# A two-layer perceiver on one core: the first cross attention begins in another order of keys, values, looks and norms

## The reference

```
x = x + _L0_xattn_ref(_layernorm(x, axis=-1), ctx_768, ...)       # x (16, 64, 256), ctx_768 (16, 1601, 192)

q = (x @ wq + bq).reshape(B, SQ, 16, 16);  k = (y @ wk + bk)...;  v = (y @ wv + bv)...
scores = jnp.einsum('bqhd,bkhd->bhqk', q, k) / jnp.sqrt(jnp.asarray(D_HEAD, x.dtype))
attn = jax.nn.softmax(scores, axis=-1)
out = jnp.einsum('bhqk,bkhd->bqhd', attn, v).reshape(B, SQ, D_EMBED);  return out @ wo + bo
```

## Time and profile before

| | |
|---|---|
| median of 3 runs | 1882.81 us (1880.94 to 1883.79) |
| span of the profiled execution | 1878.6 us |
| busy over the span | TensorE 96%, VectorE 68%, ScalarE 50%, GpSimd 49% |
| first scores of TensorE (round 0) | 45.64 us |

### The profile page before, as it was taken

How to read it: one execution, slowest core, us unless ns; L and a number is a source line. 1 busy time by engine, 2 the same in 40 slices (tenths; PEclk the granted TensorE clock), 3 DMA queues, 4 the chain that set the end, 5 groups by cost and what they waited for, 6 DMA issues and landing times.

```text
span 1878.6 us, 44195 instructions
## 1 busy us (share of the span) xinstructions
PE 1804.1 (96%) x17738; PEld 1528.4 (81%) x17738; DVE 1280.6 (68%) x2720; ACT 942.6 (50%) x2050; POOL 912.6 (49%) x1183
## 2 busy tenths in 40 slices
PE   6999999999999999999999999999999999899998
PEld 5778878887887778889999999999999967656665
DVE  6888888888888877667676666676676736652222
ACT  3676766766667745454444444444444424512221
POOL 5877777777777517455433433333333214412322
PEclk9999999999999999999999999999999999999999
DMA  5112111121110110133222222232222024141110
GB/s 161 37 48 61 37 38 37 38 67 42 37 37 3 58 50 1 58 94 105 62 62 62 62 62 62 75 86 76 73 62 62 1 97 199 36 159 29 25 32 13
DMA packets 50747, 113.08 MB, mean 60 GB/s; under 512 B 4929, under 2 KB 37265, under 8 KB 49009
## 3 DMA queue, kind: packets, MB, share of 16 engines
q1 hardware_dynamic: 46128, 105.13, 18.9%
q0 software_dynamic: 4416, 5.12, 1.6%
HBM read 105.78 MB, written 5.37 MB: 59 GB/s over the span
## 4 chain that ended last, share of the span: by engine, by line
PE 79%; DVE 10%; ACT 6%; issue 3%; DMA 2%; SPq 0%; POOL 0%; POOLq 0%; DVEq 0%; ACTq 0%
PE ps L104 8%; PE ps L164 8%; PE ps L2650 6%; PE ps L500 5%; PE ps L481 5%; PE ps L1715 5%; PE ps L458 4%; PE ps L2674 3%; PE ps L475 2%; PE ps L1716 2%; PE ps L410 2%; DVE arena L1827 2%; PE ps L1702 2%; PE ps L1705 2%; PE ps L1704 2%
## 5 line engine op out<-in xcount | busy, mean ns | idle before, releaser
L574 DVE TENSOR_REDUCE arena<-ps 128x1 f32<-128x400 f32 (+1 forms) x512 | 257.6, 565 | 84.7 <-PE ps L458 84.3
L729 ACT ACTIVATE arena<-ps 128x384 f32<-128x384 f32 (+1 forms) x512 | 223.3, 524 | 94.3 <-PE ps L481 93.9
L1715 PE MATMUL ps<-arenaR 128*128 128x386 f32 x768 | 242.9, 374 | 1.1 <-DVE arenaR L1821 1.1
L813 POOL TENSOR_TENSOR arena<-arena 128x512 f32<-128x512 f32 (+1 forms) x152 | 196.6, 1294 | 81.6 <-ACT arena L729 74.2
L1931 ACT CAST arenaR<-ps 128x512 fp32r<-128x512 f32 (+1 forms) x256 | 116.8, 509 | 199.6 <-PE ps L164 198.7
L1716 PE MATMUL ps<-arenaR 128*128 128x194 f32 x768 | 194.2, 253 | 0.0
L1821 DVE TENSOR_TENSOR arenaR<-ps,arenaR 128x512 fp32r<-128x512 f32 (+1 forms) x256 | 138.9, 585 | 28.4 <-ACT arenaR L1931 28.4
L1716 PEld LDWEIGHTS ps<-arenaR 128*128 128x128 f32 x768 | 147.5, 192 | 0.0
L1956 ACT ACTIVATE wsb<-ps,arena 128x1200 f32<-128x1200 f32 x64 | 80.9, 1265 | 131.4 <-DVE arena L1880 131.4
L1715 PEld LDWEIGHTS ps<-arenaR 128*128 128x128 f32 x768 | 145.5, 189 | 1.4 <-DVE arenaR L1821 1.4
L1827 DVE TENSOR_REDUCE arena<-ps 128x1 f32<-128x400 f32 (+1 forms) x256 | 137.1, 566 | 0.6 <-PE ps L1705 0.6
(11 more groups left out here) (374 smaller groups left out, 4948.6 us busy)
## 6 DMA issues: line engine op xcount, KB each, us to landing
wsb<-in_ctx SPq DMA_DIRECT2D x16, 1152.0 KB
wsb<-in_ctxT SPq DMA_DIRECT2D x16, 800.5 KB, 5.0
wsb<-in_ctxT SPq DMA_DIRECT2D x32, 400.2 KB, 7.5
gu<-in_m_gu SPq DMA_DIRECT2D x8, 1536.0 KB, 19.2
arena<-in_ctxT SPq DMA_DIRECT2D x15, 800.5 KB, 5.3
arena<-in_ctxT SPq DMA_DIRECT2D x30, 400.2 KB, 7.4
dn<-in_m_dn SPq DMA_DIRECT2D x8, 768.0 KB, 11.4
wsb<-in_f_w SPq DMA_DIRECT2D x2, 1024.0 KB, 6.0
```

Of the source, the lines that this page charges most:

```text
L574: e.tensor_reduce(mx4[n % 2][:, u, i:i + 1], ps[:, at("look", n, i, u), 0:400 + (i == 3)], AX.X, ALU.max).then_inc(c.maxed.at((n, i, u)), 1)
L729: e.activation(v[:, u, 0:128 * GN[s]], ps[:, at("st", n, s, u), 0:128 * GN[s]], ACT.Exp).then_inc(c.exp_a.at((x0, n, s, u)), 1)
L813: e.tensor_tensor(sums_p[0:k], sums_p[0:k], v[0:k, :, 128 * t:128 * t + 128], ALU.add).then_inc(added_p.at((n, s)), 1)
L1715: e.matmul(o, PTh[:, t, :], v[:, t, 0:386], start=(t == 0), stop=False)
```

## The change

All of it is in `latents`. FIRST is gone: the rounds begin at 0, and what stood in the rounds -3 to -1 is written out ahead of the loop, in another order on each engine.

- VectorE alone makes the low parts of the first context: `first_low(i)` has both differences, and VectorE makes block 0 before the norm of tile 0, block 1 before the first queries, 2 and 3 after them. GpSimd's loop over L837 is gone. It makes the diagonal blocks of passes 0 and 1 and then three splits of context 1.
- TensorE: keys of both head groups for block 0, then the queries; the looks stand between keys and values of the first context instead of in pairs.
- `norms = {2 * t - 2: t ...}`: tile t is normed in round 2t - 2 (0, 2, ..., 12). The bias is added tile by tile, by GpSimd in the rounds 1, 3, ..., 15.
- SP: seven tiles of x (896 KB) are loaded behind the first part of `load_raw(1)` instead of ahead of it.

```diff
-    norms = {-3: (1, 2, 3), -2: (4, 5), -1: (6, 7)}
+    norms = {2 * t - 2: t for t in range(1, NT)}
...
-    for i in range(4):
-        at("k", 0, i)
-    at("h", 0)
-    at("q", 0)
-    for i in range(2):
-        at("v", 0, i)
-    for r in range(FIRST, LAST + 1):
+    for use in (("k", 0, 0), ("h", 0), ("k", 1, 0), ("q", 0), ("v", 0, 0), ("k", 0, 1), ("v", 0, 1), ("k", 0, 2)):
+        at(*use)
+    at_look(0, 0)
...
+    for r in range(LAST + 1):
...
-        e.dma_start(c.x[:, 1:NT, :], x[:, 1:NT, :]).then_inc(c.in_x.at("x", 16), 16)
...
         load_raw(1)
+        e.dma_start(c.x[:, 1:NT, :], x[:, 1:NT, :]).then_inc(c.in_x.at("x", 16), 16)
...
     def pe(e, w):
-        for i in range(4):
-            keys(0, i)
+        keys(0, 0)
         turn_h(0)
+        keys(1, 0)
         queries(0)
-        for i in range(2):
-            vals(0, i)
-        for r in range(FIRST, LAST + 1):
+        vals(0, 0)
+        keys(0, 1)
+        vals(0, 1)
+        keys(0, 2)
+        look_at(0, 0)
+        keys(0, 3)
+        look_at(0, 1)
+        vals(0, 2)
+        look_at(0, 2)
+        vals(0, 3)
+        look_at(0, 3)
+        vals(0, 4)
+        keys(1, 1)
+        keys(1, 2)
+        turn_m(0)
+        keys(1, 3)
+        look_at(1, 0)
+        vals(0, 5)
+        look_at(1, 1)
+        vals(0, 6)
+        for r in range(LAST + 1):
...
     def dve(e, w):
+        def first_low(i):
+            k = slice(400 * i, 400 * i + 400 + (i == 3))
+            lo = c2[0][64:128, k]
+            w.wait_ge(*c.split_hi((x0, 0, i, 1)))
+            e.tensor_tensor(c1l[0][:, k], raw1[0][:, k], c1h[0][:, k], ALU.subtract).then_inc(c.dv.at(), 1)
+            w.wait_ge(*c.split_hi((x0, 0, i)))
+            e.tensor_tensor(lo, raw2[0][64:128, k], lo, ALU.subtract).then_inc(c.dv.at(("first low", i)), 1)
...
-            w.wait_ge(*c.biased(x0))
+            w.wait_ge(*c.biased((x0, tile)))
...
+        first_low(0)
         norm_tile(c, e, w, "in", 0)
+        first_low(1)
+        queries(0)
+        first_low(2)
+        first_low(3)
+        w.wait_ge(*padded("rows"))
         for i in range(4):
+            maxima(0, i)
+        maximum(0)
+        for i in range(2):
+            maxima(1, i)
+        for r in range(LAST + 1):
...
-            for t in norms.get(r, ()):
-                norm_tile(c, e, w, "in", t)
+            if r in norms:
+                norm_tile(c, e, w, "in", norms[r])
...
     def pool(e, w):
-        for i in range(4):
-            k = slice(400 * i, 400 * i + 400 + (i == 3))
-            w.wait_ge(*c.split_hi((x0, 0, i, 1)))
-            e.tensor_tensor(c1l[0][:, k], raw1[0][:, k], c1h[0][:, k], ALU.subtract).then_inc(c.split_lo.at((x0, 0, i)), 1)
         blockdiag(0)
-        for r in range(FIRST, LAST + 1):
+        blockdiag(1)
+        for i in range(3):
+            split(1, i)
+        for r in range(LAST + 1):
...
-            if r == -1:
+            if r % 2 and r // 2 < NT:
+                t = r // 2
                 w.wait_ge(*c.in_bias[0]("in"))
-                w.wait_ge(*c.normed(("in", NT - 1)))
-                e.tensor_tensor(c.x[:, :, :], c.x[:, :, :], c.biasb[:, :].unsqueeze(1).broadcast_to([128, NT, D]),
-                                ALU.add).then_inc(c.biased.at(x0), 1)
+                w.wait_ge(*c.normed(("in", t)))
+                e.tensor_tensor(c.x[:, t, :], c.x[:, t, :], c.biasb[:, :], ALU.add).then_inc(c.biased.at((x0, t)), 1)
```

More of the change, by code:

```diff
@@ L233, in latents @@
     G0, GN = (0, 4, 7, 10), (4, 3, 3, 3)
-    FIRST, LAST = -3, 2 * N
+    LAST = 2 * N
     w_hi = c.w_hi
@@ L305, in at, with at_look @@
         return bank[use]
-    for i in range(4):
-        at("k", 0, i)
-    at("h", 0)
-    at("q", 0)
-    for i in range(2):
-        at("v", 0, i)
-    for r in range(FIRST, LAST + 1):
+    def at_look(n, i):
+        for u in range(4):
+            at("look", n, i, u)
+    for use in (("k", 0, 0), ("h", 0), ("k", 1, 0), ("q", 0), ("v", 0, 0), ("k", 0, 1), ("v", 0, 1), ("k", 0, 2)):
+        at(*use)
+    at_look(0, 0)
+    at("k", 0, 3)
+    at_look(0, 1)
+    at("v", 0, 2)
+    at_look(0, 2)
+    at("v", 0, 3)
+    at_look(0, 3)
+    for use in (("v", 0, 4), ("k", 1, 1), ("k", 1, 2), ("m", 0), ("k", 1, 3)):
+        at(*use)
+    at_look(1, 0)
+    at("v", 0, 5)
+    at_look(1, 1)
+    at("v", 0, 6)
+    for r in range(LAST + 1):
         for i in range(2):
@@ L317, in latents @@
                     at("st", n, s, u)
-            for n, k in looks(r)[i:i + 1]:
-                for u in range(4):
-                    at("look", n, k, u)
+            for use in looks(r)[i:i + 1]:
+                at_look(*use)
             if r >= 1 and i == late(r):
@@ L371, in load_raw @@
                 w.wait_ge(*c.split_hi((x0, b - 2, 3)))
-                w.wait_ge(*c.split_lo((x0, b - 2, 3)))
-            if b == 2:
-                w.wait_ge(*c.dv(("first low", 3)))
+                w.wait_ge(*(c.split_lo((x0, b - 2, 3)) if b > 2 else c.dv(("first low", 3))))
             e.dma_start(raw1[b % 2], d["ctxT"][b, 0:128, :]).then_inc(in_ctx[b % 2].at(None, 16), 16)
@@ L398, in split_done @@
             w.wait_ge(*c.split_hi((x0, b, i)))
-            w.wait_ge(*c.split_lo((x0, b, i)))
-            if b == 0:
-                w.wait_ge(*c.dv(("first low", i)))
+            w.wait_ge(*(c.split_lo((x0, b, i)) if b else c.dv(("first low", i))))
         def keys(n, i):
@@ L642, in dve @@
             e.tensor_tensor(wl[k], W[k], wh[k], ALU.subtract).then_inc(c.dv.at(("weight low", k)), 1)
+        first_low(0)
         norm_tile(c, e, w, "in", 0)
-        for i in range(4):
-            k = slice(400 * i, 400 * i + 400 + (i == 3))
[L646 to L650, removed]
-        for r in range(FIRST, LAST + 1):
+        first_low(1)
[3 more added lines that the diff above has]
+        w.wait_ge(*padded("rows"))
+        for i in range(4):
+            maxima(0, i)
[3 more added lines that the diff above has]
+        for r in range(LAST + 1):
             if asks(r - 1) is not None:
@@ L655, in dve @@
                 project(projects(r - 1))
-            for t in norms.get(r, ()):
+            if r in norms:
                 w.wait_ge(*c.in_x("x"))
-                moments(c, e, w, "in", t)
+                moments(c, e, w, "in", norms[r])
             for use in looks(r)[:1]:
@@ L747, in act @@
             e.copy(wh[k], W[k]).then_inc(w_hi.at(k), 1)
-        for i in range(4):
-            split(0, i)
-        for i in range(4):
-            keys(0, i)
+        split(0, 0)
+        keys(0, 0)
         take_h(0)
-        for i in range(2):
-            vals(0, i)
-        for r in range(FIRST, LAST + 1):
+        keys(1, 0)
+        split(0, 1)
+        split(0, 2)
+        vals(0, 0)
+        split(0, 3)
+        keys(0, 1)
+        vals(0, 1)
+        keys(0, 2)
+        keys(0, 3)
+        for i in range(2, 5):
+            vals(0, i)
+        for i in range(1, 3):
+            keys(1, i)
+        split(1, 0)
+        turn_m(0)
+        keys(1, 3)
+        split(1, 1)
+        vals(0, 5)
+        split(1, 2)
+        vals(0, 6)
+        for r in range(LAST + 1):
             for use in groups(r)[:1]:
```

4 lines of the change are left out of this document (2 added, 2 removed).

## The result

The changed kernel takes 1886.53 us (median of 19 runs, 1880.85 to 1890.68) against 1882.56 (19 runs of the kernel before). The ratio is 1.002, 95% interval 1.0011 to 1.0029: about 4 us slower, small but not zero. The time lies in the predicted range (1876.5 to 1887.5), but the forecast of no change was wrong. The profiled execution has a span of 1882.6 us, 4.0 over the span before, so the trace can be read against it.

A forecast was written before the change was run, and what follows sets the result against it. TensorE was taken to bound the rounds, with idle time in the beginning. A gain of 10.2 us and a loss of 10.0 (6.6 + 2.4 + 1.0) gave -0.2, so 1882.6 us, range 1876.5 to 1887.5.

The forecast's parts named there:

- the forecast of no change: Whole kernel: gain and loss within 3.8 us of each other, 0.2%; the forecast itself, chance 0.53.
- (1): Beginning: VectorE makes all eight first low parts, about 0.5 us each without GpSimd beside it, off the path.
- (2): Beginning: TensorE's queries, now third, wait for wo, landing 7.0 us after issue, at 14.2 us.
- Step (3): Beginning: TensorE's work from the queries to its first scores takes 19.6 us at full clock; first scores at 35.4.
- The slow stretch: Beginning: 3.5 us of TensorE at half speed, as before the change, cost about 1.6 us more.
- the bound of 37.5: Beginning: latest first scores if the slow stretch lasts twice as long with 0.5 us of waits; gain 8.1.
- My reading of the chain: Beginning: TensorE's 2.97 us gap ends with looks standing nearly alone; the new order can fill that idle time.
- the wait for the root: Odd rounds: norm waits for GpSimd's root, delaying TensorE's second scores 0.7 to 1.5 us, middle 1.1, six times: 6.6.
- VectorE's lag: Rounds: VectorE's lateness carried through odd into even rounds, 0 to 1.1 us, middle 0.6, four times: 2.4.
- The rule weighed there: Rounds: started first, the norm keeps 0.41, wait 0.7 a round; by the profile row 1.5; the middle was taken.
- The dear norm: Rounds: norm always stretched to 1.22 and lag handed on; loss from 14, +5.4, 1888.2 us; chance 0.15.
- The clock in the waits: Rounds: TensorE's clock falls in waits, 1.6 us a time, more than once; waits here under 2; chance 0.03.

The follow-up runs named there:

- e6: Changed kernel, but GpSimd makes the low part of the first context again, as before; 1884.41 us in one execution.
- e3: Kernel before with its own beginning; only norms of tiles 1 to 7 and bias additions moved into the rounds; 1890.84 us, ratio 1.0036 to before.
- e9: Kernel before with its own beginning, norms in the rounds as changed, GpSimd's root first in the even round; 1879.65 us, ratio 0.998 to before.
- e12: Changed kernel with GpSimd's root at the head of the even round, run a second time; 1874.36 us, ratio 0.995 to before.
- e2: Changed kernel, but GpSimd makes the root first in the even round, ahead of its additions and scale; 1872.89 us, ratio 0.9946 to before.
- e5: Changed kernel, but GpSimd makes the next context's low parts ahead of the root in the even round; 1909.69 us in one execution.
- e10: Changed kernel, but the norms of tiles 1 to 7 write 32 of 256 columns; 1887.57 us, ratio 0.9999 to before.
- e14: Changed kernel, but GpSimd's first subtraction of the split waits for the norm; 1882.34 us, ratio 0.9998 to before.
- e8: Changed kernel with GpSimd's root first in the even round and TensorE's values of block 0 ahead of the first queries; 1874.16 us, ratio 0.9953 to before.

## Why the prediction was wrong

It forecast -10.2 + 10.0 = -0.2; the traces show -7.9 + 11.7 = +3.8. Both halves went the way the steps said; the gain was 2.3 too large and the loss 1.7 too small.

**Steps (1) and (2), the low parts and the queries.** The mechanism was right: low parts of 0.57 to 0.66 each instead of 1.26, and queries that wait for wo. That the low parts are off the path holds up to the queries; behind them e6 leaves it open. wo landed 7.8 us after its issue instead of 7.0: 0.9 of the missing gain. Over all the kernels it took 6.7 to 8.9, also with the transfers of before (6.7 in e3, 7.6 in e9), so one trace gave it to within 2 us at best.

**Step (3), 19.6 us of TensorE's work.** Mis-sized. At full clock it is 21.03 (e12): two looks with a pair of values between are 2.27 apart, not 0.85 + 1.2. I took half of a row of two looks less its end, but a look that stands alone between other products has 0.95 in its row. 1.4 of the missing gain. The slow stretch was put at 1.6 and is that, 22.61 against 21.03; that is luck in part, since over the seven profiles it costs 0 to 2.6. 15.09 + 22.61 gives 37.70, just outside the bound of 37.5.

**What made the beginning slow before.** My reading of the chain was wrong, without harm for the number. I laid the gap before 33.37 to looks whose maxima stand alone, and said that the new order fills it. Most of it was VectorE's norms between the maxima: 5.0 to 6.0 us are had by moving the norms alone (e3, e9). The chain of waits named only the maxima, since they ended last.

**The rounds: the wait for the root.** The mechanism was right to the step (root behind scale, norm, maxima, bank, second scores), and e2 and e5 move it both ways. The term was too small. I took the middle, 1.1, between a norm of 0.41 and one of 1.22; the odd rounds from 3 to 13 have the upper end, 1.60, or more, because the norm always starts in the same moment as GpSimd's subtraction and waits for all of it. The seven odd rounds' delays of the second scores sum to 11.25 instead of 6.6: five rounds of 1.6 to 2.0, round 3 with 2.55 for three small operations behind the norm, which I had counted at a part of 1 us, and round 1, where I had none, with 0.28.

**The rounds: VectorE's lag.** Too dear: 2.4 and 1.0 stood in the sum, and 0.5 came (11.74 less 11.25). I take it that VectorE's lateness is mostly TensorE's too, and that the idle time of the even rounds takes the rest; no run tests that by itself. In the changed kernel no even round's second scores are late (3.86 to 3.88).

**The rule weighed there.** By the Trainium skill ("SBUF — State Buffer", "Who interferes with whom") whoever issues first keeps the shared ports and the other blocks for the whole instruction. The traces agree with the second half (e10: 32 columns, 1.11, till the end of GpSimd's operation; e14: without the overlap 0.41). They speak against the first half, for this pair, if the start in the trace is the issue: VectorE's norm started 0.04 ahead and was the one that stood. Whether the ports are taken in the moment that the trace calls the start, no run here tells. The row had shown the same, and by the row alone the term was 6 x 1.5 = 9.0 in place of 6.6 and the sum +2.2: the right sign, though still within 0.2%. Taking a middle between a row and a rule that the row speaks against cost 2.4 of the 4.0 us by which the sum was off.

**The rivals.** The forecast itself asked for gain and loss within 3.8 us of each other, and they came out 3.8 apart. The dear norm, given 0.15, came by half: the norm is always 1.22, but the lag isn't handed on, only round 3 loses over 2.3, and the loss is 11.7 and not over 14. The clock in the waits, given 0.03, was judged too cheaply: waits of 2.5 us are in round 3, not under 2 as I wrote, and the clock fell there in five of seven profiles, though not in the one that the sum was compared with. So no rival came whole. The sum was off by 4.0: the gain was put 2.3 too large and the loss 1.7 too small, the latter being a wait put 4.65 too small against a lag put 2.9 too large.

## What to carry to other kernels

Before moving work out of a stage that idles into one that is bound, find what the moved instruction waits for there, and move that first: here six tiny GpSimd operations at the head of their round instead of behind a division turned 0.2% slower into 0.5% faster. Where one operation of another engine ends a wait and the next one of that engine is long, as the root and the subtraction here, the two collided every time, so the bad end of the range was the likely one, not the middle. When a chain names an operation that is always there (the maxima), look at what stands on the same engine just ahead of it.

## What the runs showed of the hardware

- A VectorE tensor_scalar that started 0.04 us ahead of a GpSimd tensor_tensor of 1.03 us ended just behind that one's end: it took 1.22 us for 256 columns (0.15 behind), 1.11 for 32 (0.03 behind), and 0.41 for 256 when they don't overlap.
- After waits of 1.19 to 2.88 us of TensorE in the beginning the products behind them ran at half speed for 3.4 to 5.5 us in six of the seven profiles above, and after waits of up to 3.02 us in none of the four with the values first. In e2 the row of the granted clock shows 1.00 there, while five products of values stand 0.21 apart; in e12, at full speed, 0.12:

```profile
16.44 0.41 PE L435 MATMUL ps<-arenaR 128*128 128x256 f32 x1
16.65 0.41 PE L436 MATMUL ps<-arenaR 128*128 128x256 f32 x1
16.87 0.41 PE L437 MATMUL ps<-arenaR 128*128 128x256 f32 x1
```

- The landing of one load of 256 KB among others moved by up to 2.1 us between kernels with the same transfers (6.8 us after its issue in e12, 8.9 in e8, queries at 14.12 and 16.20), as much as half of the change that was measured.
